# An attention block loop on eight Trainium2 cores: block s+1 beside block s, or block s beside block s-3

## The reference

```python
x = x + attn(layernorm(x))      # gated recurrence: xp = silu(x W_in); alpha, beta, v from xp;
                                # h = alpha*h + beta*v; (h * silu(h)) W_out
x = x + ffn(layernorm(x))
def ffn(x):
    h = rmsnorm(x)
    q = (h @ Wq + bq).reshape(b, t, 16, 64)
    k, v = split(((h @ Wdown + bdown) @ Wup + bup).reshape(b, t, 16, 128))
    att = softmax(einsum('bthd,btgd->bthg', q, k) / sqrt(64))   # over the heads g of one token
    x = x + (einsum('bthg,btgd->bthd', att, v).reshape(b, t, 1024) @ Wo + bo)
    h2 = rmsnorm(x)
    gate = softmax(h2 @ Wg + bg)
    return x + einsum('btd,edf,bte->btf', h2, We, gate)         # 8 experts, all of them, weighted
```

## Time and profile before

| | |
|---|---|
| runs of the kernel | median 4370.98 us of 3 (4324.4 to 4416.12) |
| profiled execution, own time | 4263.44 us |
| its span, slowest core (core 1) | 4261.9 us |
| spans of the eight cores | 4212.0 to 4261.9 us |
| mean granted TensorE clock of the cores | 0.741 to 0.749 |
| busy in the span: PE, DVE, ACT, GpSimd | 60%, 31%, 27%, 3% |
| DMA | 288.46 MB, mean 68 GB/s |
| matmuls of the experts, L1367 | 4096, 921.5 us busy |
| matmuls of the seven square layers | 512 each, 111.8 to 133.9 us busy |

### The profile page before, as it was taken

One profiled execution on the slowest core, in us unless ns is written; L12 is line 12 of the kernel. 1 busy time (PEld: TensorE's weight loads), 2 busy tenths in 40 slices (PEclk: granted clock), 3 DMA queues, 4 the chain that ended last, 5 costly groups with the idle time before them and its releaser, 6 DMA issues.

```text
span 4261.9 us, 38709 instructions; the slowest of 8 cores (4212.0 to 4261.9 us)
## 1 busy us (share of the span) xinstructions
PE 2550.6 (60%) x12352; PEld 1187.9 (28%) x12352; DVE 1317.5 (31%) x1944; ACT 1136.2 (27%) x2410; POOL 107.6 (3%) x128
## 2 busy tenths in 40 slices
PE   4535955359553585635965359553695536865378
PEld 1212422123221232212422124221242213422233
DVE  1333223332233321423323332233322233232432
ACT  2342024420234202342023420244202431025310
POOL 0000000000000000000000000000000000000000
PEclk9856978569785697856978569785697756987579
DMA  6411744017440175411754017440183501834026
GB/s 106 81 19 20 131 87 87 13 20 121 97 81 19 20 119 99 79 20 20 119 99 83 17 20 129 89 96 3 20 138 79 99 1 23 146 69 79 1 42 117
DMA packets 136401, 288.46 MB, mean 68 GB/s; under 512 B 4808, under 2 KB 5064, under 8 KB 136208
## 3 DMA queue, kind: packets, MB, share of 16 engines
q0 software_dynamic: 126960, 252.08, 35.1%
q1 hardware_dynamic: 9248, 33.91, 2.2%
HBM read 521.27 MB, written 16.78 MB: 126 GB/s over the span
## 4 chain that ended last, share of the span: by engine, by line
PE 42%; DMA 16%; ACT 14%; DVE 14%; issue 7%; ACTq 3%; DVEq 3%; SPq 0%; POOLq 0%
PE bank L1367 14%; DMA w<-we 8%; ACT hfm L966 6%; DMA w<-w_outT 3%; PE bank L1076 3%; PE bank L568 3%; PE bank L394 3%; PE bank L794 3%; PE bank L1308 3%; PE bank L441 3%; DMA w<-w_vT 3%; ACTq L889 2%; ACT kpot L884 2%; DVE sstat L940 2%; DVEq L1018 2%
## 5 line engine op out<-in xcount | busy, mean ns | idle before, releaser
L1367 PE MATMUL bank<-qpg,w 128*128 128x512 bf16 x4096 | 921.5, 388 | 99.8 <-DMA w<-we 50.8
L1367 PEld LDWEIGHTS bank<-qpg,w 128*128 128x128 bf16 x4096 | 404.8, 100 | 625.1 <-issue 170.2
L1340 DVE TENSOR_TENSOR qpg<-xph,ybuf 128x4096 bf16<-128x4096 bf16 x64 | 283.2, 4425 | 522.5 <-PE bank L1367 521.0
L966 ACT ACTIVATE hfm<-bank,sstat,cpf_s 128x128 bf16<-128x128 f32 x512 | 229.1, 457 | 584.0 <-DVE sstat L945 573.8
L1034 PE MATMUL bank<-hfm 128*64 128x64 bf16 x1024 | 54.5, 243 | 547.0 <-DVE hfm L1019 547.0
L1384 ACT ACTIVATE acomb<-bank 128x512 f32<-128x512 f32 x64 | 38.3, 598 | 1163.4 <-PE bank L1367 1159.2
L940 DVE TENSOR_REDUCE sstat<-bank 128x4 f32<-128x512 f32 x128 | 88.5, 692 | 467.5 <-PE bank L917 387.6
L477 PE MATMUL bank<-xph,w 128*128 128x512 bf16 x512 | 133.9, 408 | 154.9 <-DMA w<-w_vT 117.5
L568 PE MATMUL bank<-ln1g,w 128*128 128x512 bf16 x512 | 126.1, 412 | 152.6 <-DMA w<-w_outT 152.6
L1034 PEld LDWEIGHTS bank<-hfm 128*64 128x64 bf16 x1024 | 41.1, 148 | 577.3 <-issue 577.3
L868 PE MATMUL bank<-zb,wupb 64*128 64x512 bf16 x128 | 73.1, 584 | 152.0 <-ACT vpu L884 109.4
(11 more groups left out here) (137 smaller groups left out, 3134.5 us busy)
## 6 DMA issues: line engine op xcount, KB each, us to landing
w<-we POOLq DMA_DIRECT2D x64, 2048.0 KB, 14.6
w<-w_inT POOLq DMA_DIRECT2D x8, 2048.0 KB, 15.1
w<-w_aT POOLq DMA_DIRECT2D x8, 2048.0 KB, 14.2
w<-w_bT POOLq DMA_DIRECT2D x8, 2048.0 KB, 14.9
w<-w_vT POOLq DMA_DIRECT2D x8, 2048.0 KB, 13.3
w<-w_outT POOLq DMA_DIRECT2D x8, 2048.0 KB, 18.9
w<-wq POOLq DMA_DIRECT2D x8, 2048.0 KB, 33.2
w<-wo POOLq DMA_DIRECT2D x8, 2048.0 KB, 13.5
```

The source lines that it names most:

```text
L966: last_s = s.activation(out=p1_[bb % 2][:, g4 * 128:(g4 + 1) * 128], in_=bkS[:, g4 * 128:(g4 + 1) * 128], func=AF.Exp, scale=cpf2[:, C2_Q8 ...
L1340: r = v.tensor_tensor(qpg[:, (e % 2) * 4096:(e % 2) * 4096 + 4096] .rearrange("p (c q) -> p c q", q=512), h2v[:, :, :], ybuf[:, e * 512:(e ...
L1367: last_pe = pe.matmul(bk[:, :], wslice(wbuf, kc, mc), qpg[:, (e % 2) * 4096 + kc * 512: (e % 2) * 4096 + (kc + 1) * 512], start=(e == 0 an ...
```

## The change

`emit_front` is split. `emit_F1` holds `f_s1` and `f_vs`, `emit_F2` holds `f_exp`, and `emit_B` holds `f_norm` and all that was in `emit_back`. Step `step` emits F1 and F2 of block `step` and B of block `step - 3`. The probabilities, their normalised form, the laid-out V and the statistics have four slots each (`bb % 4`); the scores rotate over three banks, the V transposes over banks 5 and 6, the probability transposes over 3 and 4, and the output has bank 7 alone. All but the raw probabilities move from `hfm` to `xph2`. The factor 0.125 is taken out of the loop: the Q eviction `f_qe` gets it as a scale operand, with a bias that one multiply at the start of the program prepares, and the scaling of the maxima (L945) and the scale operand of the exponentials go. Some waits of the neighbouring stages name other events, to fit the new banks and buffers.

```diff
-    p1_ = [hfm[:, 0:512], hfm[:, 512:1024]]
-    p1n_ = [hfm[:, 1024:1536], hfm[:, 1536:2048]]
-    p1t_ = [hfm[:, 2048:2560], hfm[:, 2560:3072]]
-    vlay_ = [hfm[:, 3072:3328], hfm[:, 3328:3584]]
+    p1_ = [hfm[:, i * 512:(i + 1) * 512] for i in range(4)]
+    p1n_ = [xph2[:, i * 512:(i + 1) * 512] for i in range(4)]
+    p1t_ = [xph2[:, 2048 + i * 512: 2048 + (i + 1) * 512] for i in range(2)]
+    vlay_ = [xph2[:, 3072 + i * 256: 3072 + (i + 1) * 256] for i in range(4)]
...
+            r = v.tensor_scalar_mul(cph[:, 48:64], cph[:, 0:16], 0.125)
...
-                                     func=AF.Identity, bias=cph[:, h:h + 1])
+                                     func=AF.Identity,
+                                     scale=cpf2[0:64, C2_Q8:C2_Q8 + 1],
+                                     bias=cph[:, 48 + h:48 + h + 1])
...
-            def emit_front(bb):
-                bkS = banks[bb % 2]
-                bkV = banks[2 + bb % 2]
+            def emit_F1(bb):
+                bkS = banks[bb % 3]
+                bkV = banks[5 + bb % 2]
...
-                    if bb >= 2:
-                        pe.wait_ge(s_se.h, tok[("p1e", t, bb - 2)])
+                    else:
+                        pe.wait_ge(s_se.h, tok[("p1e", t, bb - 3)])
...
-                    if bb >= 1:
-                        v.wait_ge(s_se.h, tok[("p1e", t, bb - 1)])
-                    v.drain()
-                    v.tensor_reduce(
-                        sstat[:, S_GMAX:S_GMAX + 4],
+                    if bb >= 4:
+                        v.wait_ge(s_se.h, tok[("p1e", t, bb - 4)])
+                    v.drain()
+                    r = v.tensor_reduce(
+                        sstat[:, SG_[bb % 4]:SG_[bb % 4] + 4],
...
-                    v.drain()
-                    r = v.tensor_scalar_mul(sstat[:, S_GMAX:S_GMAX + 4],
-                                            sstat[:, S_GMAX:S_GMAX + 4], 0.125)
...
+            def emit_F2(bb):
...
+            def emit_B(bb):
+                bkP = banks[3 + bb % 2]
+                bkO = banks[7]
...
-            def emit_back(bb):
-                bkP = banks[6 + bb % 2]
-                bkO = banks[4 + bb % 2]
...
-            emit_front(0)
-            for bb in range(16):
-                if bb + 1 < 16:
-                    emit_front(bb + 1)
-                emit_back(bb)
+            DEPTH = 3
+            for step in range(16 + DEPTH):
+                if step < 16:
+                    emit_F1(step)
+                    emit_F2(step)
+                if step >= DEPTH:
+                    emit_B(step - DEPTH)
```

More of the change, by code:

```diff
@@ L120, in build_program @@
     S_GMAX, S_SSUM, S_RSUM = 44, 48, 52
+    SG_ = [64 + 4 * i for i in range(4)]
+    SS_ = [80 + 4 * i for i in range(4)]
+    SR_ = [96 + 4 * i for i in range(4)]
     banks = [ctx.enter_context(nc.psum_tensor(f"bank{i}", [128, 512], F32))
@@ L186, in pre_sync @@
             sync.dma_start(out=cpf[:, :], in_=cpf_d).then_inc(s_x.h, 16)
-            sync.dma_start(out=cph[:, :], in_=cph_d).then_inc(s_x.h, 16)
+            sync.dma_start(out=cph[:, 0:48], in_=cph_d).then_inc(s_x.h, 16)
             sync.dma_start(out=cpf2[:, :], in_=cpf2_d).then_inc(s_x.h, 16)
@@ L294, in emit_ln1_stats, with pre_bq8 @@
             block.vector(fv3)
+        def pre_bq8(v):
+            v.wait_ge(s_x.h, tok["x0"])
+            r = v.tensor_scalar_mul(cph[:, 48:64], cph[:, 0:16], 0.125)
+            s_ve.inc(r)
+        block.vector(pre_bq8)
         block.scalar(load_set(SET_LNE))
@@ L949, in f_vs @@
                     v.wait_ge(s_pe.h, tok[("vt", t, bb)])
-                    if bb >= 2:
-                        v.wait_ge(s_pe.h, tok[("av", t, bb - 2)])
+                    if bb >= 4:
+                        v.wait_ge(s_pe.h, tok[("av", t, bb - 4)])
                     v.drain()
-                    r = v.tensor_copy(vlay_[bb % 2][:, :],
+                    r = v.tensor_copy(vlay_[bb % 4][:, :],
                                       bkV[:, :].bitcast(BF16)[:, 0:256])
@@ L962, in f_exp @@
                         dwait(s, "d_hfm")
-                    if bb >= 2:
-                        s.wait_ge(s_ve.h, tok[("p1n", t, bb - 2)])
+                    if bb >= 4:
+                        s.wait_ge(s_ve.h, tok[("p1n", t, bb - 4)])
                     for g4 in range(4):
                         last_s = s.activation(
-                            out=p1_[bb % 2][:, g4 * 128:(g4 + 1) * 128],
+                            out=p1_[bb % 4][:, g4 * 128:(g4 + 1) * 128],
                             in_=bkS[:, g4 * 128:(g4 + 1) * 128],
                             func=AF.Exp,
-                            scale=cpf2[:, C2_Q8:C2_Q8 + 1],
-                            bias=sstat[:, S_GMAX + g4:S_GMAX + g4 + 1],
-                            accum_out=sstat[:, S_SSUM + g4:S_SSUM + g4 + 1])
+                            bias=sstat[:, SG_[bb % 4] + g4:SG_[bb % 4] + g4 + 1],
+                            accum_out=sstat[:, SS_[bb % 4] + g4:SS_[bb % 4] + g4 + 1])
                     s_se.inc(last_s)
@@ L975, in emit_front @@
                 block.scalar(f_exp)
+            def emit_B(bb):
+                bkP = banks[3 + bb % 2]
+                bkO = banks[7]
                 def f_norm(v, t=t, bb=bb):
                     v.wait_ge(s_se.h, tok[("p1e", t, bb)])
-                    if bb >= 2:
-                        v.wait_ge(s_pe.h, tok[("p1tT", t, bb - 2)])
+                    if bb >= 4:
+                        v.wait_ge(s_pe.h, tok[("p1tT", t, bb - 4)])
                     v.drain()
-                    v.reciprocal(sstat[:, S_RSUM:S_RSUM + 4],
-                                 sstat[:, S_SSUM:S_SSUM + 4])
+                    v.reciprocal(sstat[:, SR_[bb % 4]:SR_[bb % 4] + 4],
+                                 sstat[:, SS_[bb % 4]:SS_[bb % 4] + 4])
                     v.drain()
                     r = v.tensor_tensor(
-                        p1n_[bb % 2][:, :].rearrange("p (g n) -> p g n", n=128),
-                        p1_[bb % 2][:, :].rearrange("p (g n) -> p g n", n=128),
-                        sstat[:, S_RSUM:S_RSUM + 4]
+                        p1n_[bb % 4][:, :].rearrange("p (g n) -> p g n", n=128),
+                        p1_[bb % 4][:, :].rearrange("p (g n) -> p g n", n=128),
+                        sstat[:, SR_[bb % 4]:SR_[bb % 4] + 4]
                         .rearrange("p (g o) -> p g o", o=1)
@@ L1027, in f_av @@
                     pe.wait_ge(s_ve.h, tok[("vle", t, bb)])
[L1028 to L1031, removed]
+                    if bb >= 1:
+                        pe.wait_ge(s_ve.h, tok[("ote", t, bb - 1)])
+                    elif t > 0:
+                        pe.wait_ge(s_ve.h, tok[("G", t - 1, 7)])
                     for g4 in range(4):
```

33 lines of the change are left out of this document (22 added, 11 removed).

## The result

The change made the kernel faster: the ratio to the kernel before is 0.971, with a 95% interval of 0.968 to 0.974. The runs have a median of 4139.7 us (10 runs, 4125.5 to 4271.7) against 4298.3 of the kernel before (10 runs, 4251.7 to 4416.1). In some runs of either kernel the cores of a die have a lower granted clock and take some per cent longer; the ratio leaves these runs out on both sides, so it is not the quotient of the two medians, which is 0.963. The profiled execution took 4126.0 us, its slowest core 4124.4, where the sum of the prediction had 4125.8.

What follows compares the result with a forecast made beforehand. Hand-overs between engines were taken to bound the attention stage. Its step falls from 6.72 to 5.66 us, the stage from 107.6 to 90.4, 137.6 us over eight tiles: 4371.0 becomes 4233 us, 8 in 10 between 4150 and 4320.

Steps and rivals of the forecast that it cites:

- What leaves the ring: Attention loop, reduction to next reduction: the exponentials (1.88 us), the waits on both sides and the scaling (0.26 with gap) go.
- What enters it: Same loop: the V copy (0.37 us with its gap) and DVE's wait for the probability transposes (+0.99 us) are added.
- Term (b): Multiply and probability transposes of one block now share a step, so DVE waits for PE: +0.99 us a step.
- Ring 5.66: Attention loop, from one reduction to the next: 5.66 us a step, 1.06 less than 6.72.
- Fill and drain: Attention stage with its start and end: reduction(3) at 5.6 us, 12 steps of 5.66, three backs alone 11.7; 90.4 us against 107.6.
- a sign of being wrong: Attention loop: a new wait on ACT in steps 3 to 15 was listed among the signs that the prediction is wrong.
- Nothing behind becomes late: Stages after attention: nothing hidden becomes late, so everything behind moves up by the same 17 us a tile.
- The two scale operands: Exponentials without the operand: zero effect, even at twice 0.46 us; Q eviction with one: 0 to +0.2 us a tile.
- PE out of its low clock: Rival: PE leaves 1.2 GHz in the attention loop, 0.8 us a step, 100 in all: 4133 us; chance 0.05.
- Full overlap: Rival: the attention loop falls to DVE's own work, 3.2 us a step with gaps: 3990 us; chance 0.02.
- The round trips or the loads eat it: Rival: multiply to copy in the attention loop costs more than read, step from about 6.1 us: 4310 us; chance 0.13.
- Dense stages lose clock: Rival: matmuls of experts and square layers slow from 0.222 to 0.266 us each, +338 us: 4571 us; chance 0.04.

Runs made afterwards that it cites:

- depth1: The changed kernel with the back (normalising through output copy) one block behind the front instead of three; ratio to the kernel before 0.975.
- norm_front: The changed kernel, slots, banks and fold kept, with a block's reciprocal and multiply right behind its own reduction, rest of the back one block behind; ratio 0.983.
- order_nofold: The changed kernel with the factor 0.125 put back in the loop (scaling of the maxima, scale operand of the exponentials); ratio to the kernel before 0.976.
- all_ahead: The changed kernel with every round trip between DVE and PE put a step apart; median 3849.9 us, ratio to the kernel before 0.900.
- ote_act: all_ahead with the Q eviction's factor 0.125 as a constant and the output copy moved from DVE to ACT; median 3797.0 us, ratio to the kernel before 0.892.
- trans_ahead: The changed kernel with reciprocal and multiply one block ahead of the rest of the back; span 3993.8 us, ratio to the kernel before 0.939.

## Why the prediction was right

The direction, the mechanism and the size hold. **What leaves the ring**: shown. The exponentials and both waits around them are off it (depth1 against norm_front, which differ in the place of the normalising alone: 6.10 to 5.67), and with them off, their price does not matter (order_nofold).

**What enters it**: shown. Term (b), +0.99, is 0.97 when taken out alone, and the multiply's start to the first transpose is 0.95 in the rows of after, the transposes' start to the copy 0.81 against the 0.83 of the sum. **Ring 5.66**: measured 5.66 to 5.67.

**Fill and drain**: 90.4 us forecast, 91.0 measured, with terms that missed in both directions. The fourth reduction comes 5.1 us into the stage and not 5.6, mostly because the exponentials of block 0 take 1.51 us and not 1.88. The twelve steps behind it take 68.9 us in the mean and not 67.9; most are 5.66 to 5.71, single ones up to 6.4. The part from the last reduction to Wo takes 17.0 and not 16.9. Of the one microsecond, about 0.4 lie in the first two steps with a back, where the transposes start 0.1 to 0.2 us later behind the multiply than in the others; see the last section. The trace shows the second of them as a wait on ACT, which the prediction had named as a sign of being wrong:

```profile
1283.59 0.69 DVE L1004 TENSOR_TENSOR xph<-hfm,sstat 128x512 bf16<-128x512 bf16 x1
...
1284.75 0.59 PE L1026 MATMUL bank<-cpb_s,xph 128*128 128x128 bf16 x4 [2.58 <-ACT hfm L982]
```

Such a row stands once in every tile. The code has no wait for exponentials there; on ACT's semaphore it waits for the K and V of the tile, long done. The other long steps are single gaps of 0.1 to 0.4 us whose cause stays open. The kernel before has such steps as well (108.2 in the mean and not the 107.6 of the tile I read), 0.6 us a stage; that this cancels the 0.6 of after is in part luck, since the shorter fill hides half of the longer steps.

**Nothing behind becomes late**: the gain of the stages, 138 us, is the gain of the span, 137.5.

**The time itself** was 93 us too high: 4233 forecast, 4139.7 measured, and below the 4150 of the range. The step that failed is the base. I took the 137.6 us off the median of three runs, 4371; over ten runs that kernel has a median of 4298, and those three are among its five longest. Its profiled execution, from which the sum was made, took 4263, and off that the sum gives 4125.8 against the 4126.0 of the profiled execution of after; that these agree to 0.2 us is luck, since single runs scatter by more. As a ratio the forecast was 0.969 against 0.971 measured.

**The two scale operands** were mis-sized, with opposite signs. I bounded the exponential without its operand from above, at twice the price, and gave it no gain; it became 0.08 to 0.09 us cheaper, 457 to about 370 ns. That hardly touched this forecast (0.4 us in the fill), because ACT had left the ring; in the old order it is 0.36 us a step. And I gave the Q eviction 0 to 0.2 us a tile, for its last pair: it went from 686 to 776 ns, a pair with its hand-over is then longer than the eight matmuls beside it, and PE paces by it: a group of 16 matmuls starts 3.80 us after the one before it, where the earlier trace rows has 3.61. In the third tile the Wq layer takes 15.7 us instead of 15.1; over all eight PE waits 4.1 us for the evictions there, which is 0.5 us a tile. The two rows of the chain of after:

```profile
1227.26 3.61 PE bank L803 x16
1231.06 3.61 PE bank L803 x16
```

The Trainium skill states this price ("ScalarE: Activation LUTs", "What ACT_TABLE_LOAD costs"): each per-partition pointer operand adds about 93 ns to an ACTIVATE. Both rows of this case agree, +90 ns on the eviction and -81 to -91 ns on the exponential. I had not weighed that page.

**The rivals.** *PE out of its low clock*: not seen, 0.50 in every stage. *Full overlap*: rightly excluded for this order, by the two neighbours in DVE's queue that I named; the order all_ahead that pulls them apart reached it. *The round trips or the loads eat it*: not seen; from multiply to copy it is 1.76 us against the 1.78 of the sum, and a transfer of expert weights lands after 14.6 us in both kernels. *Dense stages lose clock*: not seen. The mean granted clock of the cores rose, 0.752 to 0.755 against 0.741 to 0.749, but it rises already because the stage at 0.50 is shorter. The test is the experts' matmuls, before and after:

```profile
L1367 PE MATMUL bank<-qpg,w 128*128 128x512 bf16 x4096 | 921.5, 388 | 99.8 <-DMA w<-we 50.8
```

```profile
L1389 PE MATMUL bank<-qpg,w 128*128 128x512 bf16 x4096 | 917.2, 386 | 95.1 <-DMA w<-we 50.7
```

They take 386 ns each and not 388, and wait for their weights as long as before.

## What to carry to other kernels

Where every engine is served in order, write down the ring, from an instruction to its successor in the next block, with each engine's turn in it, and take the time from the sum of the starts; depth and buffers help only where they let a consumer stand a step behind its producer. A producer and its consumer on another engine and back, all in one step of the same queue, cost a round trip each (about 1 us here), however many blocks are in flight: give each trip a step of its own, until the busiest queue has no bracket left. Then the next gain is to move work off that queue.

## What was not expected of the hardware

The granted clock stayed at 0.50, 1.2 GHz, in stages in which PE was busy 35.7 of 55.8 us (all_ahead) and 35.7 of 48.6 us (ote_act), 64% and 73%, with rests of about 1.0 and 0.5 us ahead of the transposes as its longest in a step. I had expected that such a loop might come out of it. The Trainium skill ("TensorE: Matmul & The Clock Gate", "What's actually happening") says that sustained activity releases the clock; in these two windows, of a loop of small matmuls and transposes, it stayed at the lower level all the same. Why was not tested.

Waits for events that are long past were not free. Ahead of the probability transposes the code of before has, for block 0, one wait in the first tile and two in the others. The code of after has three in the first tile and four in the others for blocks 0 and 1, whose banks other stages have used, and two for all later blocks. From the start of the multiply to the start of the transposes the traces have 0.84 us with one wait, 0.95 with two (in either kernel), 1.05 with three and 1.15 to 1.17 with four: about 0.1 us more for each, although all but the wait for the multiply were over long before. The prediction took its added waits at nothing. depth1, norm_front and trans_ahead show the same for block 0, 1.05 and 1.15 to 1.20. The row of one wait, block 0 of the first tile of before (the row of four is the pair shown above):

```profile
246.37 0.69 DVE L985 TENSOR_TENSOR hfm<-hfm,sstat 128x512 bf16<-128x512 bf16 x1
...
247.21 0.58 PE L1008 MATMUL bank<-cpb_s,hfm 128*128 128x128 bf16 x4 [2.81 <-DVE hfm L985]
```

No run changes the number of waits alone, so the price of one is worked out from these rows and not tested.
